# Fold stage of a ViT tokenizer: filter banks with the output channel innermost, residual products as two column halves

## The reference

```python
x = (x - mean) / (1e-06 + std) / math.sqrt(P)
x = _conv2d(x, conv1_w, conv1_b)
residual = x
x = gelu(_group_norm(x, gn1_g, gn1_b))
x = _conv2d(x, rconv1_w, rconv1_b)
x = gelu(_group_norm(x, gn2_g, gn2_b))
x = _conv2d(x, rconv2_w, rconv2_b)
x = residual + x
x = _conv2d(x, proj_w, proj_b, stride=P, pad=0)     # 192 outputs for a patch
...
h = h + attention(layernorm(h)); h = h + block(layernorm(h))
```

## Time and profile before

| | |
|---|---|
| median of 3 runs | 1872.88 us (1866.81 to 1878.74) |
| profiled execution, its time | 1862.46 us |
| its span in the trace | 1860.6 us |
| PE busy | 1711.3 us, 92% of the span |
| DVE, ACT, POOL busy | 72%, 51%, 50% |
| mean granted clock of PE | 0.967 |

### The profile page before, as it was taken

The page is one execution under the profiler, slowest core; times in us unless marked ns, Lnnn a source line. Parts: engine busy times, 40 slices in busy tenths (PEclk is TensorE's granted clock), DMA queues, the critical chain, the costliest instruction groups (busy, mean ns, idle before and its releaser), DMA issues. The chain is left out here.

```text
span 1860.6 us, 35434 instructions
## 1 busy us (share of the span) xinstructions
PE 1711.3 (92%) x8824; PEld 1082.6 (58%) x8824; DVE 1332.0 (72%) x5077; ACT 944.6 (51%) x2114; POOL 937.2 (50%) x2183
## 2 busy tenths in 40 slices
PE   7899978777999999989998999899999979788999
PEld 2344433333577567747775777477657759655657
DVE  8976767777778878878778878778878864348330
ACT  3466654555555555555555555555555550143441
POOL 2000006676676676666676677676677650133410
PEclk9999989999999999999999999999999989787989
DMA  4442332000222121212211221221122237700000
GB/s 147 145 124 85 90 132 81 19 24 20 70 69 67 46 69 48 65 51 67 67 47 48 67 69 41 75 59 56 42 76 69 65 98 194 157 1 1 1 1 14
DMA packets 51109, 124.10 MB, mean 67 GB/s; under 512 B 9167, under 2 KB 26510, under 8 KB 49062
## 3 DMA queue, kind: packets, MB, share of 16 engines
q1 hardware_dynamic: 50982, 122.52, 22.3%
HBM read 102.76 MB, written 19.69 MB: 66 GB/s over the span
## 5 line engine op out<-in xcount | busy, mean ns | idle before, releaser
L450 PE MATMUL rc<-sb_ghl,sb_rws 128*128 128x512 f16 x3528 | 1057.1, 391 | 20.1 <-ACT sb_g2f L399 17.7
L390 ACT ACTIVATE sb_f32q<-c,sb_gsh,sb_gsc 128x128 f32<-128x128 f32 x788 | 296.2, 456 | 346.0 <-POOL sb_gsh L344 346.0
L450 PEld LDWEIGHTS rc<-sb_ghl,sb_rws 128*128 128x128 f16 x3528 | 343.8, 104 | 161.9 <-issue 38.9
L338 POOL TENSOR_TENSOR sb_tmp<-sb_tmp,sb_half_neg 128x4 f32<-128x4 f32 (+1 forms) x296 | 403.3, 1362 | 23.2
L399 ACT ACTIVATE sb_g2f<-rc,sb_gsh,sb_gsc 128x128 f32<-128x128 f32 x784 | 295.6, 467 | 185.6 <-POOL sb_gsh L344 169.9
L333 POOL TENSOR_TENSOR sb_tmp<-sb_mst 128x4 f32<-128x4 f32 (+1 forms) x296 | 72.5, 245 | 518.1 <-DVE sb_mst L722 515.5
L510 PE MATMUL pj<-sb_wall,sb_arena 128*112 128x384 f16 x896 | 299.3, 341 | 10.1 <-DVE sb_arena L746 8.9
L511 PEld LDWEIGHTS pj<-sb_wall,sb_arena 128*112 128x112 f16 x896 | 243.5, 272 | 90.6 <-issue 3.6
L510 PEld LDWEIGHTS pj<-sb_wall,sb_arena 128*112 128x112 f16 x896 | 243.2, 271 | 40.2 <-DVE sb_arena L746 9.0
L746 DVE TENSOR_TENSOR sb_arena<-sb_g2f,sb_arena 128x512 f32 (+1 forms) x196 | 136.6, 697 | 151.3 <-ACT sb_arena L407 137.6
L511 PE MATMUL pj<-sb_wall,sb_arena 128*112 128x192 f16 x896 | 223.5, 249 | 0.0
(11 more groups left out here) (152 smaller groups left out, 1798.2 us busy)
## 6 DMA issues: line engine op xcount, KB each, us to landing
sb_wall<-w_lo SPq DMA_DIRECT2D x28, 1008.0 KB, 4.9
sb_im<-x_planes SPq DMA_DIRECT2D x300, 60.7 KB
sb_wall<-w_lo SPq DMA_DIRECT2D x14, 1056.0 KB, 4.9
sb_im<-x_planes SPq DMA_DIRECT2D x300, 30.3 KB
sb_f32q<-in_proj SPq DMA_DIRECT2D x12, 576.0 KB, 4.2
sb_arena<-in_proj SPq DMA_DIRECT2D x12, 576.0 KB, 4.7
w_lo<-sb_arena SPq DMA_DIRECT2D x1, 6144.0 KB, 17.1
scratch_fold<-sb_wall SPq DMA_DIRECT2D x24, 247.5 KB
```

Of the source, the lines that this page charges most:

```text
L338: ch.did(gp.tensor_tensor(t5, t3, half_neg[:, 0:w], ALU.pow))
L390: ins = nc.scalar.activation(g1f[:, q * Q + m, :], c1[q][:, m * HALF:(m + 1) * HALF], ACT.Gelu, bias=gsh[q][:, m:m + 1], scale=gsc[q][:, m ...
L450: last = nc.tensor.matmul(out, w[:, wp, 3 * t + m, :], v[:, xp, q * Q:q * Q + Q, t:t + 8, m:m + P], start=(n == 0), stop=(n == 17))
```

## The change

It has four parts. The matmuls of the filter banks write their 512 columns in the same order as before, but to addresses in the bank that have the channel innermost: the columns of one channel go to every fourth fp32 word (`"p (n e) -> p e n"`). The two evictions then read the bank from end to end and store four neighbouring channels at a time, where they stored one channel's 128 positions one after the other. The residual product of eight channels and 384 columns on 55 partitions becomes two products of four channels and 192 columns each, with weights padded to 64 columns, one into partitions 0 to 63 and one into 64 to 127 of the same bank; ACT evicts 128x192 in place of 55x384. The store of `tev` becomes two transfers, one for each half, and the waits on it count 32 in place of 16.

```diff
-TR = 55
+TR, TP = 55, 64
...
-        wv = wlo[0:TR, :, :, :].rearrange("p a b c -> p (a b c)").bitcast(F32)
-        tev = [wv[:, i * U * DENSE:(i + 1) * U * DENSE].rearrange("p (e n) -> p e n", e=U) for i in range(2)]
+        wv = wlo[:, :, :, :].rearrange("p a b c -> p (a b c)").bitcast(F32)
+        tev = [wv[:, i * Q * DENSE:(i + 1) * Q * DENSE].rearrange("p (e n) -> p e n", e=Q) for i in range(2)]
...
                     sp.wait_ge(s_psp, 2 * n + 2)
                     load_proj(n + 2, p)
                 sp.wait_ge(s_tev, 3 * n + 3)
-                sp.dma_start(bass.AP(tensor=ts.tensor, offset=n * (U * TR * DENSE),
-                                     ap=[[DENSE, TR], [TR * DENSE, U], [1, DENSE]]),
-                             tev[p][:, :, :]).then_inc(s_ts[p], 16)
+                for h in range(2):
+                    sp.dma_start(bass.AP(tensor=ts.tensor, offset=n * (U * TR * DENSE) + h * (Q * TR * DENSE),
+                                         ap=[[DENSE, TR], [TR * DENSE, Q], [1, DENSE]]),
+                                 tev[p][TP * h:TP * h + TR, :, :]).then_inc(s_ts[p], 16)
 
             with sp.Fori(0, 3) as i:
                 for p in range(2):
...
                                  ).then_inc(s_tc[m % NTC], 16)
 
 
-            sp.wait_ge(s_ts[0], 16 * (FU // 2))
-            sp.wait_ge(s_ts[1], 16 * (FU // 2))
+            sp.wait_ge(s_ts[0], 32 * (FU // 2))
+            sp.wait_ge(s_ts[1], 32 * (FU // 2))
             load_chunk(GROUPS, 0)
             load_chunk(GROUPS, 1)
             for e in range(2):
...
                 n = 2 * i + p
                 for q in range(2):
                     act.wait_ge(s_fold, 2 * n + q + 1)
-                    nc.scalar.activation(whi[:, :, bass.ds(n * U + q * Q, Q)].rearrange("p n e -> p e n"),
-                                         rc[p][q][:, :].rearrange("p (e n) -> p e n", e=Q),
+                    nc.scalar.activation(whi[:, :, bass.ds(n * U + q * Q, Q)],
+                                         rc[p][q][:, :].rearrange("p (n e) -> p n e", e=Q),
                                          ACT.Copy, scale=1.0 / WS).then_inc(s_whi, 1)
                 if not first:
-                    act.wait_ge(s_ts[p], 16 * i)
+                    act.wait_ge(s_ts[p], 32 * i)
                 act.wait_ge(s_tps, n + 1)
                 for k, bank in enumerate((c1[0], c1[1], pj)):
                     nc.scalar.activation(tev[p][:, :, 3 * P * k:3 * P * (k + 1)],
-                                         bank[0:TR, 0:384].rearrange("p (e n) -> p e n", e=U),
+                                         bank[:, 0:192].rearrange("p (e n) -> p e n", e=Q),
                                          ACT.Copy, scale=1.0 / (WS * WS)).then_inc(s_tev, 1)
 
             act.wait_ge(s_wprep, W_READY)
...
                 for q in range(2):
                     if not first:
                         pe.wait_ge(s_wlo, 2 * (n - 2) + q + 1)
-                    run(bands(rc[p][q][:, :], fws, ghl[p], q)).then_inc(s_fold, 1)
+                    run(bands(rc[p][q][:, :].rearrange("p (n e) -> p e n", e=Q), fws, ghl[p], q)).then_inc(s_fold, 1)
                 if not (first and p == 0):
                     pe.wait_ge(s_tev, 3 * n)
                 v = ghl[p][:, :, :].rearrange("p h (g r w) -> p h g r w", g=U, r=SL)
                 for k, bank in enumerate((c1[0], c1[1], pj)):
                     for m, (wp, xp) in enumerate(((0, 0), (0, 1), (1, 0))):
-                        last = nc.tensor.matmul(bank[0:TR, 0:384], tws[:, wp, :], v[:, xp, :, 3 * k:3 * k + 3, 1:17],
-                                                start=(m == 0), stop=(m == 2))
+                        for h in range(2):
+                            last = nc.tensor.matmul(bank[TP * h:TP * h + TP, 0:192], tws[:, wp, :],
+                                                    v[:, xp, Q * h:Q * h + Q, 3 * k:3 * k + 3, 1:17],
+                                                    start=(m == 0), stop=(m == 2))
                 last.then_inc(s_tps, 1)
 
             pe.wait_ge(s_wprep, W_READY)
...
                 for q in range(2):
                     dve.wait_ge(s_whi, 2 * n + q + 1)
                     sl = bass.ds(n * U + q * Q, Q)
-                    v.scalar_tensor_tensor(wlst[:, :, sl].rearrange("p n e -> p e n"),
-                                           rc[p][q][:, :].rearrange("p (e n) -> p e n", e=Q), 1.0 / WS,
-                                           whi[:, :, sl].rearrange("p n e -> p e n"), ALU.mult,
+                    v.scalar_tensor_tensor(wlst[:, :, sl], rc[p][q][:, :].rearrange("p (n e) -> p n e", e=Q), 1.0 / WS,
+                                           whi[:, :, sl], ALU.mult,
                                            ALU.subtract).then_inc(s_wlo, 1)
 
             dve.wait_ge(s_padz, 2)
```

More of the change, by code:

```diff
@@ L130, in build_front @@
         n += 1536
-        tws = b0[:, n:n + 2 * TR].rearrange("p (h m) -> p h m", h=2)
-        n += 2 * TR
+        tws = b0[:, n:n + 2 * TP].rearrange("p (h m) -> p h m", h=2)
+        n += 2 * TP
         w1hl = b0[0:KC, n:n + 256].rearrange("p (h m) -> p h m", h=2)
@@ L137, in build_front @@
         stage = [f32q[:, :], b1[:, HALF * E:HALF * E + 2 * U * DENSE].bitcast(F32)]
-        wv = wlo[0:TR, :, :, :].rearrange("p a b c -> p (a b c)").bitcast(F32)
-        tev = [wv[:, i * U * DENSE:(i + 1) * U * DENSE].rearrange("p (e n) -> p e n", e=U) for i in range(2)]
+        wv = wlo[:, :, :, :].rearrange("p a b c -> p (a b c)").bitcast(F32)
+        tev = [wv[:, i * Q * DENSE:(i + 1) * Q * DENSE].rearrange("p (e n) -> p e n", e=Q) for i in range(2)]
         wst = whi[:, 0:24, :].rearrange("p a c -> p (a c)").bitcast(F32)
         rst32, fst32 = wst[:, 0:768], wst[:, 768:1536]
-        tst32, w1st32 = wst[:, 1536:1536 + TR], wst[0:KC, 1600:1728]
+        tst32, w1st32 = wst[:, 1536:1536 + TP], wst[0:KC, 1600:1728]
         xsm = g2f[0:ROWS, :, :].rearrange("p a b -> p (a b)")
@@ L1463, in layout @@
     w1 = tokp["conv1_w"]
-    tb = np.zeros((2, CH, TR), w1.dtype)
+    tb = np.zeros((2, CH, TP), w1.dtype)
     for half in range(2):
         tb[half, :, 27 * half:27 * half + 27] = w1.reshape(CH, 27)
-    o["tband"] = tb.reshape(128, TR)
+    o["tband"] = tb.reshape(128, TP)
     wb = np.zeros((KC, 2, CH), w1.dtype)
```

## The result

The changed kernel takes 2006.95 us (median of 4, 2001.14 to 2015.54) against 1871.22 us in the same comparison: 1.0725 times the time before, 95% interval 1.0665 to 1.0784. Its profiled execution took 2011.93 us, with a span of 2010.1 us, 149.5 more than before.

What follows compares the result with a forecast made beforehand. PE bounds the kernel (92% busy), evictions hidden in the loop. Filters +167.7, residual halves -20.4, gap ahead of step 6 -6.0, end -1.8 sum to +139.5: 2002 us profiled, 2012 us median, range 1838 to 2035.

Steps and rivals of the forecast that it cites:

- rival A: Strided bank is free for the fold's filter matmuls, kernel gets faster: -29.0 us, 1844 us on the median; chance 0.27.
- Half rate for the stepped bank: Fold's filter matmuls: two clocks a column, 0.429 us each, a step's filter part 15.4 us; chance 0.60.
- The sum: Whole kernel: filters +167.7, residual products -20.4, idle time -6.0, end -1.8, together +139.5 us.
- The halves: Residual products in each fold step: pairs run at once, 0.95 us in place of 1.80, 20.4 us less in 24 steps.
- The gap ahead of step 6 and the end: PE's idle time ahead of fold step 6 goes entirely, -6.0 us; last filter matmul to patches -1.8 us.
- The evictions: Filter evictions by ACT and DVE in runs of four: 0.9 us each; worth nothing in the loop.
- Rival B: Nearly no change, 1864 us: 0.253 us a filter matmul, or free bank with halves one after the other; chance 0.10.
- Rival C: Worse than half rate: the step costs 3.2 times, 0.73 us a filter matmul, 2277 us; chance 0.03.

## Why the prediction was right

It forecast 2012 us and 1.0725 was measured, 2007. The total tests the sum only roughly: +139.5 was forecast, the medians differ by 135.7, the profiled executions by 149.5, and in the fold, where the change acts, it is +144.2. Nor does the stated range say much, since it holds rival A as well. What makes the prediction right is its decisive term. Step by step:

- *Half rate for the stepped bank.* The decisive term, taken from the bounds as 0.429 us a matmul, measured 0.432. It was argued from steps elsewhere on the chip, and given no more than 0.60. The reason given, that PSUM takes two neighbours at a time, held in the experiments in a more exact form: the two that PE reads together must be neighbours.
- *The sum.* +167.7 was forecast for the filters, +172.5 measured. Of the missing 4.8 us, 2.5 are the matmul's 0.432 in place of 0.429, over 864 of them. The other 2.3 are the first step: the sum took 0.429 us there as well, though PE starts it at its lower clock. Taken so, half rate costs nothing as long as the clock is low. It does cost. In the first 4.3 us of the fold the trace has 11 filter matmuls before and 6 after:

```profile
13.70:18.00 4.30, 4.30 (x11) 1.48 (x12) 1.84 (x2) 0.00 (x0) 0.00 (x0) 1.00 1.04 289
82.58:85.00 2.42, 2.42 (x6) 0.84 (x7) 2.42 (x2) 0.00 (x0) 0.00 (x0) 0.50 1.02 299
...
13.70:18.00 4.30, 4.30 (x6) 1.16 (x7) 1.85 (x2) 0.00 (x0) 0.00 (x0) 1.00 1.02 264
```

(These are windows, two of the kernel before and one of the changed kernel: length, busy time and count of PE, PEld, DVE, ACT and POOL, clock, DMA share, GB/s.) The clock column says 1.00 in the first 4.3 us, but the starts of the matmuls say otherwise: before they lie 0.427 us apart there, just as from 82.58 us on, where the column gives 0.50, and in the changed kernel 0.853. So the first step took 17.81 - 15.55 = 2.3 us more than the others. A stepped column costs two clocks of PE at either level, not a fixed time.

- *The halves.* Expected 0.95 us for the residual part, measured 0.98; 19.7 us in place of 20.4. Reading the overlap off an unlike matmul (fp32, 294 columns) was sound.
- *The gap ahead of step 6 and the end.* Gone entirely as forecast, and 2.4 in place of 1.8 us at the end: the three residual evictions of the last step overlap and take 0.8 us in all, where 1.5 had been taken.
- *The evictions.* 0.60 and 0.69 us, where 0.9 was taken. On ACT, runs of four are as fast as the copy with adjacent output (0.63 us).
- *Rival A* (free bank, 1844 us) is out for the change as made. The version with the bank written in a row shows what its sum was worth. It takes 1845.9 us, but that is luck in part: by the ratio it gains 21 us, where A had 29.0, and the time before was 5 us lower in that comparison. The path was wrong too. The idle time isn't 1.4 us ahead of step 6, it is 9 us ahead of step 8, behind the SP queue, which I had looked at only for its number of issues. With the stores spread it is 1831.6.
- *Rival B* needed 0.253 us a matmul, or a free bank with the halves in line; 0.432 was measured, and the halves alone take 0.98 us a step. *Rival C* has nothing for it: 16 bytes cost no more than 8.

The Trainium skill's rule ("PSUM — Partial Sum Buffer", Specifications: lines of 8 bytes, any pattern that isn't contiguous slows matmuls significantly) was right for the step of four and of two. The runs differ from it elsewhere: a jump after every two or four columns costs nothing where the moving operand begins on an even element (0.218 us a matmul, as with a bank in a row). "Advanced Engine Details and Errata", section Memory Cachelines, has a sentence that fits all of them: "Every two consecutive elements should be contiguous for best throughput."

## What to carry to other kernels

If a PSUM result has to be transposed on its way to SBUF, put the step into the reading of PSUM, not into PE's output: here the step cost PE 7.3 us in each of 24 steps and the readers nothing. Ask of a speedup which engine sets the pace first: the evictions were hidden in the loop, and 1.9 us saved on each bought 0.3% with the SP queue as it was and 0.94%, 17.6 us, with its stores spread, both times with the short residual part. What they would bring with the old residual part and a bank in a row, no run shows. And where a faster engine is the aim, look at what its loads are queued behind.

## What the runs showed of the hardware

- A matmul whose neighbouring output columns aren't neighbours in PSUM takes two clocks a column: 0.432 us for 512 at a step of 8 or 16 bytes, against 0.22 to 0.23. At the lower clock it doubles as well, from 0.427 to 0.853. Here it makes no difference whether the moving operand begins on an even element: 0.43 us both ways.
- Twos count as they are read. With an odd fp16 start of 16-element runs: 0.247 us into a bank in a row, 0.312 with a jump after four columns, 0.392 after two; with even starts 0.221 even with a jump after every two. The first of these agrees with reading in twos: an odd run of 16 takes nine reads in place of eight, and 9/8 of 0.218 gives 0.245 as an estimate. Why the last of the odd ones is 0.392 and not 0.43, as 16 single writes for 16 columns would give, stays open.
- Two fp16 matmuls of 64 output rows on the two column halves run at once: nine pairs of 192 columns and the switching in 0.98 us.
- Storing one fp16 every 384 bytes costs ACT 4.9 and DVE 5.1 ns an element, in runs of four 1.2 and 1.35; their reading of PSUM with a step of 512 bytes costs the same as in a row.
